# Landing pieces up to four cells wide in three slots of 32 KB, in place of three cells in four slots of 24 KB

## The chip, the cores and the metric

The kernel runs on one core of a Trainium2 chip. Its time is device microseconds (us) of one execution. Three timed runs of the kernel before took 1202.51, 1204.64 and 1207.39 us, so the median is 1204.64 us. The engines are TensorE (PE; its weight loads are PEld), VectorE (DVE), ScalarE (ACT), GpSimd (POOL) and SyncE (SP); SP only issues DMAs here. "ACTq" and "SPq" are the sequencers of ScalarE and SyncE, where DMAs are issued and semaphores waited for.

## The reference

One layer of a graph network. The adjacency matrix is dense in memory (268 MB) although it is almost empty, and every entry is used as an ordinary number:

```python
x    : (8192, 128) f32, normal        adj : (8192, 8192) f32, almost all zeros, diagonal 0.05..1
W    : (128, 128) f32

h       = max(layernorm(x, axis=-1), 0)
A_hat   = adj + eye(8192)
d       = sum(A_hat, axis=1) ** -0.5
A_norm  = d[:, None] * A_hat * d[None, :]
out     = x + relu(A_norm @ (h @ W.T))
```

The degrees `d` need the sum over a whole row of `adj` before any product with that row's part of `h @ W.T` can be taken.

## The kernel before

The matrix is cut into 16 x 16 **cells**. Cell (u, v) is rows of block u against columns of block v, 512 x 512 numbers, 1 MB. Block row u is called **stripe** u. The kernel goes through the stripes once, in order s = 0 to 15, and in stripe s it loads:

- `far[s]`: the cells right of the band (v > s + 1). They are loaded for the row sums alone. ScalarE sums them (L530) and they are thrown away. One piece takes `MOST * B` = 12 cells-wide rows of one quarter of the block rows, or several quarters when fewer cells are left (L87 to L94).
- `left[s]`: the cells v < s, in **pieces** of up to `MOST` cells (`split`, L73). VectorE transposes them (L692), TensorE multiplies the transposed cells with `support` (L485), and both VectorE (L677) and ScalarE (L540) take a part of the row sums.
- `near[s]`: the cells s and s + 1, in two buffers of their own.
- `early[s]`: cells of earlier rows that had been summed before and can now be multiplied, because the scale of their columns is known. These are loaded a second time, always three cells in a piece (L101).

After stripe 15 the cells that are still missing are loaded a second time, in pieces of up to `MOST` cells (`AGAIN_ROWS`, L107). In all the kernel reads 387 MB.

All pieces but `near` are numbered m = 0, 1, 2, ... in one list, `landing`. Piece m goes to buffer `slot[m % SLOTS]`. Both DMA queues load every piece: SP its partitions 0 to 63, ScalarE its partitions 64 to 127, two DMAs each for pieces of cells (`load_cells`, L266). A DMA's rows are n x 512 bytes long for a piece of n cells.

What sets the order: `next_piece` (L518). When ScalarE comes to piece m and it has landed, it first issues its half of piece m + `AHEAD`, and only then sums piece m. Before it issues, `load_piece` (L285) makes it wait until the piece that was in that slot has been used: `act_freed` and `dve_freed` for a piece that is summed, `t_done` (the transposes) for a second load. SP may issue its half once ScalarE has passed the same point (`act_piece`). With `AHEAD = SLOTS - 1`, the piece waited for is m - 1, in both kernels. After the last piece of a stripe, `load_kept` (L306) issues `near`, and waits first until the transposes of the column s - 1 have begun to use the other buffer. From stripe 10 on this column stands behind the first four cells of the stripe (`FIRST`, L133). After stripe 15 nothing is summed, and a slot is reloaded when the transposes of its piece are done.

VectorE transposes a cell in two halves into three buffers `adjT` (`TURNS`), so it runs at most three halves ahead of TensorE. A cell is two transposes and eight matmul instructions.

Of the kernel before, what the change touches and what calls it, by code (L numbers as in the profile page):

```python
# [28 lines left out]
def gnn_kernel(nc: bass.Bass, x: bass.AP, adj: bass.AP, w: bass.AP, out: bass.AP):  # L29
# [8 lines left out]
    C = G // Q  # L38
    CELL = N // B // NB
    BAND = 1  # L40
    MOST = 3
    SLOTS = 4
    AHEAD = 3
    HALVES = 2
    TURNS = 3
    BANKS = 5
# [26 lines left out]
    def split(first, end):  # L73

        n = end - first
        k = -(-n // MOST)
        return [(first + n * i // k, n * (i + 1) // k - n * i // k) for i in range(k)] if n > 0 else []
# [4 lines left out]
    landing = []  # L82
    far, left, again, early = {}, {}, {}, {}
    next_cell = [u + BAND + 1 for u in range(FAR_ROWS)]
    middle = []
    for u in range(NB):
        cells = NB - 1 - u - BAND  # L87
        far[u] = []
        widths = [] if cells <= 0 else [cells] if cells <= MOST * B else [MOST * B, cells - MOST * B]
        for k, width in enumerate(widths):  # L90
            per = min(B, MOST * B // width)
            for bb in range(0, B, per):
                far[u].append(len(landing))
                landing.append(("far", u, bb, min(per, B - bb), NB - cells + k * MOST * B, width))  # L94
        left[u] = []
        for v, n in split(0, u):
            left[u].append(len(landing))
            landing.append(("left", u, v, n, 0, 0))
        early[u] = []
        if u <= EARLY_TO:  # L100
            for i in range(u - MOST - BAND - 1, -1, -MOST):  # L101
                early[u].append(len(landing))
                middle.append((i, u - MOST))
                landing.append(("again", i, u - MOST, MOST, 0, 0))
                next_cell[i] = u
    AGAIN = len(landing)
    for u in AGAIN_ROWS:  # L107
# [4 lines left out]

    slot_of = [m % SLOTS for m in range(len(landing))]
    before_in_slot, landed = [], []
# [30 lines left out]
    def group(u, v):  # L145

        if v <= u + BAND:
            return "row", u
        if v >= next_cell[u]:
            return "end", AGAIN_ROWS.index(u)  # L150
        return "middle", middle.index((u, v - (v - u - BAND - 1) % MOST))

    def bank_of(g):
        kind, k = g
# [20 lines left out]
    with ctx:  # L175
# [17 lines left out]
        acc = sb("acc", [D, FAR_ROWS, G])  # L193
        slot = [sb(f"slot{i}", [P, MOST * C * CELL]) for i in range(SLOTS)]
        near = [sb(f"near{i}", [P, C, 2 * CELL]) for i in range(2)]
# [312 lines left out]
        def _(act):  # L508
# [9 lines left out]
            def next_piece(m):  # L518

                load_piece(act, (2, 3), m + AHEAD)  # L520
                if m + AHEAD in last_piece:
# [340 lines left out]
```

## Time and profile before

| | |
|---|---|
| timed runs | 1202.51 to 1207.39 us, median 1204.64 us |
| profiled execution | span 1237.8 us from first to last instruction; no time of its own beside the span |
| TensorE busy | 983.2 us (79%), 2365 instructions |
| VectorE busy | 802.4 us (65%), 965 instructions |
| ScalarE busy | 586.5 us (47%), 1735 instructions |
| DMA | 391.81 MB, mean 317 GB/s, the 16 engines busy in nearly every slice |
| granted TensorE clock, mean | 0.909 |
| cells | 256, of which 101 are multiplied before 676 us and 155 after |

How to read it: the share of an engine over the whole span hides that the kernel has two halves. The page's slices show TensorE at 3 to 8 tenths in the first half and at 9 from 700 us on, while the DMA engines show 9 nearly everywhere. "Busy" for TensorE includes the modelled ends of its matmuls. The DMA share is the time packets took, so a full queue of slow packets shows as busy as one of fast packets: the GB/s column tells them apart.

### The profile page before, as it was taken

The numbers are of one execution on the slowest core, as the hardware profiler recorded it, in microseconds if no ns is written. First come the engines' busy times: TensorE is split into PE (matmuls) and PEld (weight loads), VectorE is DVE, ScalarE is ACT, GpSimd is POOL, SyncE is SP. The second block draws the span as 40 slices with busy tenths as digits, with TensorE's granted clock in tenths as the row PEclk, the third lists the DMA queues.
The fourth block names the chain that finished last, engine by engine and source line by source line (L and its number), as shares of the span: only waits on it lengthen the run. The fifth ranks groups of instructions, "written<-read, shape, count | busy, mean of one in ns | idle before, by whom it ended". The sixth has DMA issues, their size and how long they took to land.

```text
span 1237.8 us, 9242 instructions
## 1 busy us (share of the span) xinstructions
PE 983.2 (79%) x2365; PEld 451.8 (36%) x2365; DVE 802.4 (65%) x965; ACT 586.5 (47%) x1735; POOL 52.6 (4%) x61
## 2 busy tenths in 40 slices
PE   0633346566687788796597999999999999899997
PEld 0631122222233333342243444444444444344443
DVE  5342233444476566575485888888888888778775
ACT  2797587776384637145254451724715653010011
POOL 3000000000000000000000000000000000010001
PEclk9767668678889899998798999999999999999999
DMA  9989999999999999999999999999999997999993
GB/s 301 380 320 309 392 398 362 365 369 347 362 349 343 362 337 322 314 256 274 281 291 278 329 332 360 323 276 333 309 325 320 314 271 215 271 271 348 337 328 88
DMA packets 275204, 391.81 MB, mean 317 GB/s; under 512 B 10832, under 2 KB 252624, under 8 KB 275152
## 3 DMA queue, kind: packets, MB, share of 16 engines
q1 hardware_dynamic: 137648, 195.65, 51.3%
q10 hardware_dynamic: 137504, 195.58, 50.5%
q8 instruction: 19, 0.31, 0.1%
q14 instruction: 33, 0.27, 0.1%
HBM read 386.99 MB, written 4.19 MB: 316 GB/s over the span
## 4 chain that ended last, share of the span: by engine, by line
PE 37%; DMA 8%; ACT 6%; ACTq 3%; DVE 1%; issue 0%; POOLq 0%; SPq 0%; DVEq 0%
PE bank L485 36%; DMA slot<-in_adj_dram 8%; ACT junk L540 6%; ACTq L269 2%; DVE adjT L692 1%; ACTq L277 1%; PE pre L461 0%; ACTq L315 0%; DVE near L778 0%; ACT slot L530 0%; ACT near L558 0%; DVE part L677 0%; POOLq L175 0%; PE sums_bank L449 0%; ACTq L321 0%
## 5 line engine op out<-in xcount | busy, mean ns | idle before, releaser
L485 PE MATMUL bank<-adjT,support 128*128 128x512 f32 x2048 | 936.2, 618 | 152.1 <-DVE adjT L692 150.8
L692 DVE STREAM_TRANSPOSE adjT<-slot 128x1024 f32<-128x1024 f32 x450 | 546.5, 1233 | 268.8 <-DMA slot<-in_adj_dram 157.2
L485 PEld LDWEIGHTS bank<-adjT,support 128*128 128x128 f32 x2048 | 401.8, 199 | 664.6 <-issue 661.0
L540 ACT ACTIVATE junk<-slot 128x384 bf16<-128x384 f32 (+2 forms) x540 | 254.6, 473 | 196.1 <-issue 131.3
L530 ACT ACTIVATE slot<-slot 128x6144 f32<-128x6144 f32 (+11 forms) x64 | 191.8, 2998 | 250.3 <-issue 147.8
L558 ACT ACTIVATE near<-near,dinv 128x128 f32<-128x128 f32 x64 | 20.4, 390 | 177.9 <-issue 88.5
L540 ACT ACTIVATION_READ_ACCUMULATOR junk<-slot 128x1 f32 x540 | 100.8, 187 | 0.0
L692 DVE STREAM_TRANSPOSE adjT<-near 128x1024 f32<-128x1024 f32 x62 | 74.8, 1231 | 19.0 <-PE bank L485 19.0
L540 ACT ACTIVATE junk<-near 128x256 bf16<-128x256 f32 (+1 forms) x192 | 75.5, 394 | 2.8 <-ACT junk L540 2.8
L677 DVE TENSOR_REDUCE part<-slot 128x4 f32<-128x1536 f32 (+2 forms) x45 | 69.0, 1533 | 0.0
L407 POOL TENSOR_TENSOR dinv<-total,power 128x4 f32<-128x4 f32 x16 | 16.1, 1007 | 942.0 <-DVE total L746 942.0
L449 PE MATMUL sums_bank<-by_block,spread 128*128 128x64 f32 x32 | 7.1, 310 | 50.1 <-DVE by_block L728 50.1
L428 PE MATMUL bank<-ident,acc 128*128 128x128 f32 x64 | 14.9, 378 | 31.5 <-ACT acc L515 31.5
L540 ACT ACTIVATION_READ_ACCUMULATOR junk<-near 128x1 f32 x192 | 35.8, 187 | 0.0
L436 PE MATMUL bank<-acc 128*128 128x128 f32 x128 | 23.5, 344 | 9.1 <-DVE acc L645 9.0
L718 DVE TENSOR_REDUCE folded<-part 128x16 f32<-128x32 f32 (+5 forms) x16 | 3.7, 228 | 41.3 <-ACTq L589 40.9
L449 PEld LDWEIGHTS sums_bank<-by_block,spread 128*128 128x128 f32 x32 | 6.7, 228 | 58.9 <-DVE by_block L728 53.6
L416 POOL TENSOR_TENSOR near<-near 128x512 f32<-128x512 f32 x16 | 20.3, 1270 | 174.2 <-ACT near L558 154.4
L515 ACT ACTIVATE acc<-support,acc 128x128 f32<-128x128 f32 x64 | 25.4, 479 | 2.2 <-PE bank L428 2.2
L436 PEld LDWEIGHTS bank<-acc 128*128 128x128 f32 x128 | 22.3, 261 | 9.7 <-DVE acc L645 9.7
L677 DVE TENSOR_REDUCE part<-near 128x4 f32<-128x1024 f32 (+1 forms) x16 | 18.6, 1160 | 8.0 <-DMA near<-in_adj_dram 8.0
L428 PEld LDWEIGHTS bank<-ident,acc 128*128 128x128 f32 x64 | 11.2, 198 | 32.8 <-ACT acc L515 17.5
(53 smaller groups left out, 179.1 us busy)
## 6 DMA issues: line engine op xcount, KB each, us to landing
slot<-in_adj_dram SPq DMA_DIRECT2D x118, 768.0 KB, 15.4
slot<-in_adj_dram ACTq DMA_DIRECT2D x118, 768.0 KB, 13.4
slot<-in_adj_dram ACTq DMA_DIRECT2D x56, 512.0 KB, 11.0
slot<-in_adj_dram SPq DMA_DIRECT2D x56, 512.0 KB, 12.0
slot<-in_adj_dram ACTq DMA_DIRECT2D x12, 1536.0 KB, 15.8
slot<-in_adj_dram SPq DMA_DIRECT2D x12, 1536.0 KB, 17.0
near<-in_adj_dram SPq DMA_DIRECT2D x30, 512.0 KB, 16.8
near<-in_adj_dram ACTq DMA_DIRECT2D x30, 512.0 KB, 15.2
```

Of the source, the lines that this page charges most:

```text
L269: queue.dma_start(piece(m)[b * Q:(b + 1) * Q, :, :], adj_v[u, b, :, :, v * CELL:(v + n) * CELL]).then_inc(ld_slot[slot_of[m]], 16)
L407: nc.gpsimd.tensor_tensor(dinv[:, u * R:(u + 1) * R], total[:], power[:, :R], ALU.pow).then_inc(root_ok, 1)
L416: nc.gpsimd.tensor_tensor(o[n % 2], y[n % 2], xin[n % 2], ALU.add).then_inc(o_ok, 1)
L428: ins = nc.tensor.transpose(hT_bank[b % 2][:, r * P:(r + 1) * P], h[b % 2][:, r, :], ident[:])
L436: ins = nc.tensor.matmul(sup_bank[b % 2][:, r * D:(r + 1) * D], hT[b % 2][:, r * P:(r + 1) * P], wT[:], start=True, stop=True)
L485: ins = nc.tensor.matmul(bank[bank_of(g)][:], support[:, v * R + t, :], adjT[at % TURNS][:, r, :], start=(n == first_of[g] and t == 0), st ...
L515: nc.scalar.activation(h[b % 2][:, r, :], support[:, t, :], ACT.Relu, bias=shift[:, t:t + 1], scale=rstd[:, t:t + 1]).then_inc(h_ok, 1)
L530: ins = nc.scalar.activation(far_block(m)[:, a, :], far_block(m)[:, a, :], ACT.Copy, accum_out=far_sum[u % 2][:, at:at + 1])
L540: nc.scalar.activation(junk[at % JUNKS][:, :n], cells[:, c, :], ACT.Copy, accum_out=part[u % 2][:, k, c:c + 1]).then_inc(junk_done, 1)
L558: ins = nc.scalar.activation(y[n % 2][:, r, :], y[n % 2][:, r, :], ACT.Relu, scale=dinv[:, t:t + 1])
L677: return nc.vector.tensor_reduce(part[u % 2][:, k, :most], cells[:, :most, :], AX.X, ALU.add)
L692: nc.vector.transpose(adjT[at % TURNS][:].rearrange("p t (c i) -> p t c i", i=Q), half.rearrange("p c (t r) -> p t c r", r=Q)).then_inc(t_ ...
```

## The change

Four constants are changed and one is added. `MOST` goes from 3 to 4, `SLOTS` from 4 to 3, `AHEAD` from 3 to 2. The size of a slot follows `MOST`, so it grows from 24 to 32 KB in each partition, and the slots together stay at 96 KB. `EARLY = 3` is new, and keeps the second loads within the stripes (`early`) at three cells. What `MOST` still governs becomes wider: far pieces hold up to 16 cells' width, and `left` pieces and the second loads after stripe 15 hold up to four cells.

```text
                         before                          after
pieces in all            128                             108
four-cell pieces         0                               20 (16 left, 4 after stripe 15)
far[0] (quarters x width) 4 of 1x12, 1 of 4x2            4 of 1x14
far[1]                   4 of 1x12, 1 of 4x1             4 of 1x13
far[6], far[7]           4 of 1x8, 4 of 1x7              2 of 2x8, 2 of 2x7
far[9], far[10]          2x5 2x5, 3x4 1x4                3x5 1x5, 4x4
left[4]                  2 2                             4
left[7], left[8]         2 2 3, 2 3 3                    3 4, 4 4
left[10], left[11]       2 3 2 3, 2 3 3 3                3 3 4, 3 4 4
left[12], left[13]       3 3 3 3, 2 3 2 3 3              4 4 4, 3 3 3 4
left[14], left[15]       2 3 3 3 3, 3 3 3 3 3            3 4 3 4, 3 4 4 4
early (all stripes)      18 pieces of 3                  the same
```

```diff
--- before.py
+++ after.py
@@ -38,9 +38,10 @@
     C = G // Q
     CELL = N // B // NB
     BAND = 1
-    MOST = 3
-    SLOTS = 4
-    AHEAD = 3
+    MOST = 4
+    EARLY = 3
+    SLOTS = 3
+    AHEAD = 2
     HALVES = 2
     TURNS = 3
     BANKS = 5
@@ -98,10 +99,10 @@
             landing.append(("left", u, v, n, 0, 0))
         early[u] = []
         if u <= EARLY_TO:
-            for i in range(u - MOST - BAND - 1, -1, -MOST):
+            for i in range(u - EARLY - BAND - 1, -1, -EARLY):
                 early[u].append(len(landing))
-                middle.append((i, u - MOST))
-                landing.append(("again", i, u - MOST, MOST, 0, 0))
+                middle.append((i, u - EARLY))
+                landing.append(("again", i, u - EARLY, EARLY, 0, 0))
                 next_cell[i] = u
     AGAIN = len(landing)
     for u in AGAIN_ROWS:
@@ -148,7 +149,7 @@
             return "row", u
         if v >= next_cell[u]:
             return "end", AGAIN_ROWS.index(u)
-        return "middle", middle.index((u, v - (v - u - BAND - 1) % MOST))
+        return "middle", middle.index((u, v - (v - u - BAND - 1) % EARLY))
 
     def bank_of(g):
         kind, k = g
```

The same instructions in the order of ScalarE's program, stripe 12. `L277`/`L278` are loads of far pieces, `L269`/`L270` loads of pieces of cells (`32x16x384` is three cells, `32x16x512` four), `L315`/`L316` the load of `near`; the other rows are sums. Lines after the change are one higher. Before:

```order
L277 DMA slot<-in_adj_dram 128x2x256 x4
L269 DMA slot<-in_adj_dram 32x16x384 x6
L530 ACTIVATE slot,far_sum<-slot 128x1024 x4
L269 DMA slot<-in_adj_dram 32x16x384 x2
L315 DMA near<-in_adj_dram 32x16x256 x2
L540 ACTIVATE junk,part<-slot 128x384 x12
L269 DMA slot<-in_adj_dram 32x16x384 x2
L540 ACTIVATE junk,part<-slot 128x384 x12
L269 DMA slot<-in_adj_dram 32x16x384 x2
L540 ACTIVATE junk,part<-slot 128x384 x12
L269 DMA slot<-in_adj_dram 32x16x384 x2
L540 ACTIVATE junk,part<-slot 128x384 x12
```

After:

```order
L278 DMA slot<-in_adj_dram 128x2x256 x4
L270 DMA slot<-in_adj_dram 32x16x512 x4
L531 ACTIVATE slot,far_sum<-slot 128x1024 x4
L270 DMA slot<-in_adj_dram 32x16x512 x2
L316 DMA near<-in_adj_dram 32x16x256 x2
L541 ACTIVATE junk,part<-slot 128x512 x12
L270 DMA slot<-in_adj_dram 32x16x384 x2
L541 ACTIVATE junk,part<-slot 128x512 x12
L270 DMA slot<-in_adj_dram 32x16x384 x2
L541 ACTIVATE junk,part<-slot 128x512 x12
L541 ACTIVATE junk,part<-near 128x256 x12
```

Before, three pieces (x6) are issued between the far load and the far sum of stripe 12; after, two pieces (x4). The `near` load stands in the same place, ahead of the sums of the stripe's first left piece.

The same engine at the end of stripe 4, before:

```order
L277 DMA slot<-in_adj_dram 128x2x1280
L530 ACTIVATE slot,far_sum<-slot 128x5120
L269 DMA slot<-in_adj_dram 32x16x256 x2
L530 ACTIVATE slot,far_sum<-slot 128x5120
L269 DMA slot<-in_adj_dram 32x16x256 x2
L315 DMA near<-in_adj_dram 32x16x256 x2
L530 ACTIVATE slot,far_sum<-slot 128x5120
L277 DMA slot<-in_adj_dram 128x2x1152
L530 ACTIVATE slot,far_sum<-slot 128x5120
L277 DMA slot<-in_adj_dram 128x2x1152
L540 ACTIVATE junk,part<-slot 128x256 x12
L277 DMA slot<-in_adj_dram 128x2x1152
```

After:

```order
L278 DMA slot<-in_adj_dram 128x2x1280
L531 ACTIVATE slot,far_sum<-slot 128x5120
L278 DMA slot<-in_adj_dram 128x2x1280
L531 ACTIVATE slot,far_sum<-slot 128x5120
L270 DMA slot<-in_adj_dram 32x16x512 x2
L316 DMA near<-in_adj_dram 32x16x256 x2
L531 ACTIVATE slot,far_sum<-slot 128x5120
L278 DMA slot<-in_adj_dram 128x2x1152
L531 ACTIVATE slot,far_sum<-slot 128x5120
L278 DMA slot<-in_adj_dram 128x2x1152
L541 ACTIVATE junk,part<-slot 128x512 x12
L541 ACTIVATE junk,part<-near 128x256 x12
```

The two pieces of two cells have become one of four. It is loaded where the second of the two was, after the stripe's second far sum and together with `near`; in the place of the first one the fourth far piece of the stripe is loaded, one sum later than before.

## Rows read from the trace of the kernel before

**Rows 1.** Stretches (columns: stretch, length, busy per engine (x instructions), PEclk, DMA share, GB/s).
```profile
0.00:676.00 676.00, 437.71 (x1041) 206.92 (x1041) 347.60 (x481) 390.10 (x970) 26.30 (x39) 0.84 1.03 332
676.00:1229.00 553.00, 544.85 (x1320) 244.44 (x1320) 452.85 (x481) 193.85 (x757) 23.79 (x20) 0.99 1.01 301
...
500.00:600.00 100.00, 72.07 (x155) 30.79 (x153) 52.95 (x53) 39.31 (x111) 1.01 (x1) 0.88 1.03 265
```

**Rows 2.** Waits from 0 to 676 us (waiter <- releaser: us, times, longest).
```profile
DVE adjT L692 <- DMA slot<-in_adj_dram: 153.8, 26, 15.3
...
PE bank L485 <- DVE adjT L692: 136.5, 28, 12.6
```

**Rows 3.** Waits from 676 to 1229 us.
```profile
PE bank L485 <- DVE adjT L692: 14.3, 5, 8.3
DVE adjT L692 <- DMA slot<-in_adj_dram: 13.1, 3, 9.7
```

**Rows 4.** Groups of instructions by line, 676 to 1229 us, TensorE.
```profile
L485 PE MATMUL bank<-adjT,support 128*128 128x512 f32 x1240 | 539.4, 595 | 15.6 <-DVE adjT L692 14.3 <-ACT acc L552 1.4
```

**Rows 5.** Stretches with one width of row on the queues.
```profile
126.00:146.00 20.00, 10.74 (x20) 4.99 (x20) 6.64 (x15) 10.03 (x26) 1.01 (x1) 0.59 1.02 417
334.00:348.00 14.00, 7.23 (x11) 2.75 (x10) 4.74 (x4) 3.71 (x2) 0.00 (x0) 0.76 1.07 362
387.00:397.00 10.00, 6.92 (x17) 2.82 (x16) 5.01 (x6) 0.86 (x2) 0.00 (x0) 1.00 1.10 346
930.00:945.00 15.00, 15.00 (x36) 6.65 (x35) 12.78 (x14) 5.50 (x22) 0.00 (x0) 1.00 1.07 359
```

**Rows 6.** Groups by line and shape, whole span, ScalarE's sums of far pieces.
```profile
L530 ACT ACTIVATE slot<-slot 128x6144 f32<-128x6144 f32 x12 | 63.8, 5321 | 35.1 <-issue 23.3 <-DMA slot<-in_adj_dram 10.3 <-ACT junk L540 1.5
...
L530 ACT ACTIVATE slot<-slot 128x1024 f32<-128x1024 f32 x8 | 8.3, 1044 | 23.5 <-DMA slot<-in_adj_dram 22.9 <-issue 0.6
...
L530 ACT ACTIVATE slot<-slot 128x512 f32<-128x512 f32 x8 | 4.9, 617 | 23.8 <-DMA slot<-in_adj_dram 23.1 <-issue 0.6
```

**Rows 7.** Chain, 600 to 700 us (start us, us, what): two ScalarE sums.
```profile
620.60 4.91 ACT junk L540 x24
...
627.37 6.19 ACT junk L540 x24
```

**Rows 8.** Order of time, VectorE, 673 to 680 us.
```profile
675.40 2.37 DVE L692 STREAM_TRANSPOSE adjT<-slot 128x1024 f32<-128x1024 f32 x2 [9.65 <-DMA slot<-in_adj_dram]
```

**Rows 9.** L269 issued from 1012 to 1014 us: one three-cell piece, nothing queued before it.
```profile
L269 ACTq DMA_DIRECT2D slot<-in_adj_dram x2: 604/731/858, 1012.5 to 1013.1; - x2
L269 SPq DMA_DIRECT2D slot<-in_adj_dram x2: 579/710/841, 1012.5 to 1013.1; - x2
...
DMA to landing us min/median/max: 7.0/9.2/11.1
```

**Rows 10.** Order of time, ScalarE, 440 to 472 us.
```profile
449.05 9.10 ACTq L315 DMA_DIRECT2D near<-in_adj_dram  x2
```

**Rows 11.** Order of time, ScalarE, 753 to 800 us.
```profile
759.12 4.54 ACTq L269 DMA_DIRECT2D slot<-in_adj_dram  x2
770.02 2.84 ACTq L315 DMA_DIRECT2D near<-in_adj_dram  x2
...
779.37 1.56 ACTq L269 DMA_DIRECT2D slot<-in_adj_dram  x2
...
787.43 1.56 ACTq L269 DMA_DIRECT2D slot<-in_adj_dram  x2
...
795.49 2.74 ACTq L269 DMA_DIRECT2D slot<-in_adj_dram  x2
```

**Rows 12.** Order of time, VectorE, 798 to 848 us.
```profile
820.08 1.25 DVE L692 STREAM_TRANSPOSE adjT<-slot 128x1024 f32<-128x1024 f32 x1 [0.40 <-PE bank L485]
...
830.38 1.25 DVE L692 STREAM_TRANSPOSE adjT<-slot 128x1024 f32<-128x1024 f32 x1 [0.40 <-PE bank L485]
...
842.39 4.63 DVE L692 STREAM_TRANSPOSE adjT<-slot 128x1024 f32<-128x1024 f32 x4 [1.71 <-DMA slot<-in_adj_dram]
```

## The prediction

> **What bounds the kernel now.** I read the stretches first. Up to 676 us TensorE is busy 438 of 676 us and the DMA share is 1.03; from 676 us on TensorE is busy 545 of 553 us, at a DMA share that is still 1.01 [rows 1]. The waits say the same: in the first part VectorE waits 153.8 us for landing pieces and TensorE 136.5 us for VectorE [rows 2]; in the second part these are 13.1 and 14.3 us [rows 3]. So the time before is 676 us in which the queues set the pace, and 553 us in which TensorE does: 1240 matmul instructions, eight to a cell, are 155 cells, and 553 / 155 = 3.57 us a cell [rows 4]. A second taken from the first part shows in the end time. In the second part only a new wait of TensorE does, and a gain of the queues is worth nothing there.
>
> The second part is not far from the other bound. A cell of three-wide pieces is 1.05 MB, and at 359 to 362 GB/s [rows 5] takes 2.9 us, against TensorE's 3.57; but each stripe adds `near` and a far piece that feed TensorE little or nothing. So the queues have some per cent to spare, and idle time on them beyond that turns into waits of TensorE.
>
> The profiled span, 1237.8 us, is 33 us over the median of the runs, 1204.64. The stretch 500 to 600 us moved only 265 GB/s at a share of 1.03 [rows 1], where the same kind of pieces moves 360: slow packets, not missing ones. I take the sum below as a difference to the span (1237.8 + x) and carry x over to the median.
>
> **The change part by part.**
>
> *Wider rows before 676 us.* Rows of 1024 B moved at 346 GB/s, of 1536 B at 359 to 362, the long rows of far pieces at 417 [rows 5]. Rows of 2048 B do not stand alone anywhere. Bounds: 362 (no gain over three cells) and 417 (as far rows). I take 370, near the row of the nearest width. A piece of 4.19 MB then takes 11.3 us (11.6 and 10.1 at the ends), one of three cells (3.15 MB) 8.7, one of two (2.10 MB) 6.1. Stripe 4: 12.2 becomes 11.3, 0.9 saved. Stripe 7: 20.9 becomes 20.0, 0.9. Stripe 8: 23.5 becomes 22.6, 0.9. Stripe 10: 29.6 becomes 28.7, 0.9. Together 3.6 us, with the five pieces at the ends 2.1 and 9.6. Far cells: 2.1 MB of stripe 0 go from 1024 B rows to 7168 B rows, 6.1 to 5.0 us; stripe 1 has 1.05 MB of 512 B rows, which I price as 1024 B rows, 3.0 to 2.5. That is 1.6 us. On ScalarE, which is late there, four sums of 1044 ns and four of 617 become wider sums elsewhere: a sum's price is 190 ns plus 0.835 ns a column (5321 and 1044 ns) [rows 6], so only the 8 x 0.19 = 1.5 us go; half of that I put on the path. Sum: -6 us, ends -3 and -12. Merging far pieces in stripes 6 and 7 leaves rows and bytes as they were: 0.
>
> The Trainium skill, page DMA: Bandwidth & Descriptors, section Where 436 GB/s comes from, has loads from HBM bound at about 358 GB/s a core; by it rows over 1024 B would be worth 3% at most. The trace does not agree: 417 GB/s over 20 us [rows 5].
>
> *The first piece of stripe 11.* At 675.40 VectorE starts on a piece of two cells that it had waited 9.65 us for, and from there TensorE hardly stops [rows 8]. After the change this piece has three cells and lands (3.15 - 2.10) MB / 362 GB/s = 2.9 us later: +2.9 us, ends 0 (if TensorE is full earlier) and +3.
>
> *One piece less in flight, first part.* Before, ScalarE at piece m issues m + 3 while m + 1 and m + 2 are on the queues; after, m + 2 while only m + 1 is. A three-cell piece issued onto an empty queue landed 11.1 us after its last DMA's issue at 1013.1, the first being issued at 1012.5: 11.7 us, of which the bytes are 8.7 and 3.0 are latency [rows 9]. So the queue stays full only if ScalarE comes to piece m less than (time of m + 1) - 3.0 us after its landing: 5.7 us of room for three cells, 8.3 for four, about 3 for the far pieces of stripes 3 to 5. ScalarE's work fits: a sum over three cells takes 6.19, over two 4.91 us [rows 7], so four would be 7.5 us (each cell adds 1.28), plus 1.5 us to issue (779.37) [rows 11], against 8.7 and 11.3 us on the queues. And part of its lateness goes away: with more than two pieces queued an issue blocks, 9.10 us for the `near` of stripe 8 (449.05) [rows 10], 4.54 us for a third piece (759.12) [rows 11]. Nine stripe ends are left where `near` (waits for a column) or a free slot makes it late. Ends: 0, and the full 3.0 us at each of nine ends, +27. I take half a microsecond an end: +4.
>
> *One slot less, second part.* This is the largest term. At a stripe's end come three early pieces, the far piece of the next stripe, then its left pieces A and B. The far piece holds a slot and gives TensorE nothing. With three slots A may be issued once the second last early piece is transposed, B once the last one is. VectorE ends these two 10.3 us apart (820.08 and 830.38, the last transposes of the two pieces before stripe 13) [rows 12]. A is wanted when the last early piece is through: 10.3 us after its issue, and it needs 11.7 us with three cells, 11.3 + 3.0 = 14.3 with four. Late by 1.4 or 4.0. With four slots it had one piece more, 10.3 us, to spare. Stripe 11 is 3, 4, 4: A 1.4, B then another 2.6. Stripe 12 is 4, 4, 4: A 4.0, then B has 13.8 us and is in time. Stripe 13 is 3, 3, 3, 4: A 1.4, and B, issued 10.3 us after A and wanted 10.3 us after A landed, is in time. Together 9.4 us; stripes 14 and 15 have no far piece. VectorE's lead of up to three halves over TensorE absorbs what is under about 2 us once, but the queues in this part also have slow spells: at 842.39 even four slots ran dry for 1.71 us [rows 12]. I take +8, ends +2 and +15. ScalarE's place does not matter here: its `near` issue in stripe 12 already waits from 763.7 (759.12 + 4.54) to 770.02, and stands at the same sum after the change [rows 11].
>
> *After stripe 15* the widths are 2, 3, 1, 2, 3, 2, 2, 3, 3, 2, 3, 3, then 4, 3, 4, 3, 4, 4. A slot is asked for again after three pieces. A three-cell piece behind two pieces of three cells together has 3 x 3.57 = 10.7 us plus what VectorE leads, against 11.7; all others have over 14. 0, end +3.
>
> *Nothing:* ScalarE's fewer sums and VectorE's nine fewer L677 lie under the queues in the first part and under TensorE in the second.
>
> Sum: -6 + 2.9 + 4 + 8 = +9. Span 1247, timed 1213.6; I say 1213.
>
> **The rivals.** *A, gains and losses cancel:* the width gain is 6 to 8 us and the stalls of the second part are swallowed by VectorE's lead, -7 + 3 + 2 + 2 = 0: about 1205. For it: only 20 of 108 pieces have four cells, and all early pieces stay at three, so the change reaches little on either side.
>
> *B, faster:* four-cell rows go at the rate of far rows, -12, ScalarE freed from blocked issues keeps the queue as full as before, and left pieces of four arrive with as much room as three did: -12 + 2.9 + 1 + 1 = -7, about 1197. It decides from 400 GB/s on in stretches of four-cell pieces. Against it: 1024 to 1536 B brought under 5% [rows 5]. In a sentence of its own: the Trainium skill, page Perfetto Trace Analysis, section DMA Optimizations, says that DMAs under 2 KB carry much overhead and that batching them up helps dramatically; the step from 346 to 362 GB/s is this trace's measure of it.
>
> *C, much slower:* a slot less makes the queue dry at every stripe end, because ScalarE stands blocked before the `near` issue (6.3 us in stripe 12) with one piece in flight instead of two. From a block of 5.7 us on the queue dries; nine stripe ends at 3 us and six at 4 less the 6 gained give about +40, 1245. Against it: the block stands only from stripe 10 on, and the piece in flight there has four cells.
>
> *That it doesn't do what it says* is excluded by the order of ScalarE's program: four-cell loads are there.
>
> **How the numbers follow.** A measurement of this kernel can tell about 0.5% (6 us) from no change. Forecast 0.38, its own range 1211 to 1226; A 0.32; B 0.22; C 0.08. The range of 8 in 10 takes all of A, half of B and none of C: 1197 to 1231. Faster (under 1198.6) 0.22, within 0.5% 0.33, slower 0.45 (forecast and C, less the lower edge of the forecast).
>
> **What would show it.** Width: a stretch of four-cell pieces alone, 370 GB/s (B: over 400). Depth, first part: the waits of VectorE for pieces before the last turn to TensorE-bound stay near 150 us; C has them over 180. Second part: waits of VectorE for `slot` pieces over the last 155 cells go from 13 us to 20 or more, in rows at the first left pieces of stripes 11, 12 and 13; if they are not there, the largest term is wrong. If the turn comes more than 5 us earlier and the waits stay at 13, B is right. A change of the rate of three-cell pieces, which no term here has, would make all of it wrong.

## The result, and the profile after

The changed kernel took 1235.74 us (median of 4 runs, 1231.32 to 1240.91), the kernel before in the same comparison 1206.01 us (4 runs, 1202.51 to 1207.39): a ratio of 1.0249, 95% interval 1.0203 to 1.0294. The same kernel again (run e13 below) took 1231.70 us, ratio 1.0201 (1.0103 to 1.0299). The forecast was 1213 us, 1197 to 1231: the side is right, the size is not. Some 30 us were lost and 8 forecast.

The profiled execution of before that the prediction rests on had a span of 1237.8 us. A second one of the same kernel (run e0) has 1207.6, and the stretch with 265 GB/s [rows 1] moves 337 there. All comparisons below are with this second one. Its stretches, cut where TensorE begins to be full (653 us) and around the part after stripe 15:

```profile
0.00:653.00 653.00, 441.53 (x1054) 209.97 (x1055) 353.95 (x489) 396.06 (x978) 26.30 (x39) 0.84 1.04 347
653.00:1208.00 555.00, 540.42 (x1313) 242.88 (x1312) 449.32 (x478) 190.42 (x757) 26.29 (x22) 0.99 1.01 297
500.00:600.00 100.00, 86.38 (x195) 37.78 (x195) 71.64 (x75) 46.75 (x140) 2.01 (x2) 0.93 1.07 337
1003.00:1141.00 138.00, 133.39 (x338) 61.06 (x338) 107.39 (x137) 13.00 (x41) 13.65 (x11) 0.99 1.05 298
```

The same view of the changed kernel (columns as in [rows 1]). The next three stretches hold mostly four-cell pieces, and answer to [rows 5]; the last holds long far rows with a two-cell piece among them:

```profile
0.00:683.00 683.00, 466.06 (x1106) 219.66 (x1107) 372.28 (x503) 393.12 (x898) 27.33 (x40) 0.84 1.02 343
683.00:1239.00 556.00, 525.82 (x1261) 234.32 (x1259) 429.56 (x451) 170.06 (x607) 25.33 (x21) 0.98 0.96 283
1022.00:1172.00 150.00, 138.31 (x337) 62.40 (x338) 107.46 (x137) 12.68 (x40) 12.43 (x10) 0.95 0.99 277
...
447.00:467.00 20.00, 15.40 (x27) 6.25 (x26) 8.30 (x8) 5.60 (x4) 0.00 (x0) 0.76 1.06 369
655.00:675.00 20.00, 19.72 (x46) 9.11 (x47) 17.34 (x25) 2.52 (x10) 1.01 (x1) 0.92 1.06 370
742.00:750.00 8.00, 8.00 (x21) 3.78 (x20) 6.11 (x9) 0.00 (x0) 1.01 (x1) 0.91 1.05 360
...
130.00:150.00 20.00, 9.55 (x16) 3.90 (x16) 4.35 (x4) 11.97 (x5) 0.00 (x0) 0.67 1.03 391
```

The reader is to see two things. The price of four-cell rows was about right: 369, 370 and, in a shorter stretch, 360 GB/s, where 370 was taken. And in the third row, from 1022 to 1172 us, in a part that the prediction priced at nothing, TensorE stands for 12 of 150 us (before, for 4.6 of 138), and the same instructions (337 and 338 in the records) are busy for 138.3 us where they took 133.4 before. The waits, first part and second, answering to [rows 2, 3], and then, of the second part, what falls after stripe 15 (from 1022 us):

```profile
PE bank L486 <- DVE adjT L693: 149.8, 24, 17.8
DVE adjT L693 <- DMA slot<-in_adj_dram: 144.1, 15, 20.8
...
DVE adjT L693 <- DMA slot<-in_adj_dram: 28.7, 8, 8.9
...
PE bank L486 <- DVE adjT L693: 22.1, 11, 7.5
...
DVE adjT L693 <- DMA slot<-in_adj_dram: 16.2, 5, 5.7
```

In e0 VectorE's waits for pieces are fewer than in [rows 2, 3]: 120.6 us up to 653 us, and 0.7 us in all the rest.

```profile
DVE adjT L692 <- DMA slot<-in_adj_dram: 120.6, 21, 15.4
```

To see where the time goes I take, in each profile, when TensorE starts the first of the eight matmul instructions of a cell, cells counted in the order of the program. The order of the 256 cells is the same in all kernels here. The rows are us against run e0, whose own times stand first:

| run | cell 40 | 83 (stripe 10) | 101 (11) | 123 (12) | 146 (13) | 203 (rest) | 223 | 240 | last end |
|---|---|---|---|---|---|---|---|---|---|
| e0, before | 392.1 | 574.5 | 646.9 | 725.1 | 804.5 | 1003.1 | 1081.3 | 1141.4 | 1198.3 |
| after | +8.6 | +11.2 | +8.4 | +15.3 | +18.7 | +19.0 | +25.4 | +31.0 | +31.5 |
| e13, after again | +1.5 | +5.3 | +1.1 | +8.6 | +13.8 | +14.1 | +19.8 | +27.1 | +27.1 |
| e1, three slots of three | +18.3 | +27.1 | +28.1 | +34.7 | +36.9 | +46.6 | +55.2 | +57.5 | +59.6 |
| e7, far as before | +16.2 | +23.8 | +20.9 | +28.3 | +32.5 | +32.8 | +42.1 | +48.3 | +49.2 |
| e17, far joined as before | +5.3 | +10.8 | +8.2 | +16.5 | +21.0 | +21.2 | +30.0 | +36.6 | +38.0 |
| e6, three slots first | +26.4 | +28.7 | +29.4 | +29.4 | +29.4 | +29.2 | +27.7 | +29.3 | +31.3 |
| e3, rest in threes | +6.6 | +7.1 | +3.1 | +10.3 | +14.3 | +15.0 | +21.3 | +23.6 | +25.1 |
| e11, stores later | -1.1 | +0.7 | -3.5 | +3.0 | +6.9 | +7.2 | +5.7 | +12.2 | +12.2 |
| e16, both of these | -2.4 | -0.7 | -5.1 | +1.0 | +5.3 | +5.6 | +4.1 | +5.1 | +5.1 |
| e10, three slots in the rest | +3.3 | +2.0 | -1.2 | -1.7 | -1.6 | -1.5 | +5.8 | +8.8 | +10.4 |
| e15, both kernels | +4.8 | +3.4 | -2.4 | -3.3 | -3.3 | -3.8 | -3.6 | -3.6 | -3.6 |

Five of these profiles (after, e13, e3, e11, e16) run the same program up to stripe 11, and stand there between -5.1 and +8.4, median +1.1. So a difference of several us between two single profiles in this part, which the queues bound, can be the execution's own. From stripe 11 on the five agree: from cell 101 to 203 they lose 10.6, 13.0, 11.9, 10.7 and 10.7 us.

### The profile page after: what moved, and what is told of

Same layout as the page of the kernel before. It is cut to its first block, busy times and chain, and to the rows that moved or that the text cites. A ratio compares the mean times of both kernels' runs of the same rounds, so it can differ in the third digit from the quotient of the medians.

```text
span 1239.1 us, 8874 instructions
## 1 busy us (share of the span) xinstructions
PE 991.9 (80%) x2365; PEld 454.0 (37%) x2365; DVE 801.8 (65%) x954; ACT 563.2 (45%) x1503; POOL 52.7 (4%) x61
## 4 chain that ended last, share of the span: by engine, by line
PE 43%; DMA 17%; DVE 4%; ACTq 1%; ACT 1%; issue 1%; SPq 1%; POOLq 0%; POOL 0%; DVEq 0%
PE bank L486 42%; DMA slot<-in_adj_dram 16%; DVE adjT L693 3%; DMA out_dram<-near 1%; ACTq L316 1%; ACTq L270 1%; ACT junk L541 0%; DVE part L678 0%; ACT near L559 0%; ACT slot L531 0%; PE pre L462 0%; SPq L270 0%; DVE near L779 0%; SPq L322 0%; SPq L329 0%
## 5 line engine op out<-in xcount | busy, mean ns | idle before, releaser
L486 PE MATMUL bank<-adjT,support 128*128 128x512 f32 x2048 | 946.9, 624 | 171.9 <-DVE adjT L693 171.9
L693 DVE STREAM_TRANSPOSE adjT<-slot 128x1024 f32<-128x1024 f32 x450 | 547.5, 1234 | 299.8 <-DMA slot<-in_adj_dram 172.8
L486 PEld LDWEIGHTS bank<-adjT,support 128*128 128x128 f32 x2048 | 406.0, 201 | 690.6 <-issue 685.5
L541 ACT ACTIVATE junk<-slot 128x384 bf16<-128x384 f32 (+3 forms) x432 | 234.4, 544 | 206.8 <-issue 131.1
L531 ACT ACTIVATE slot<-slot 128x7168 f32<-128x7168 f32 (+13 forms) x56 | 190.2, 3397 | 247.3 <-issue 119.9
L693 DVE STREAM_TRANSPOSE adjT<-near 128x1024 f32<-128x1024 f32 x62 | 74.0, 1226 | 15.4 <-PE bank L486 15.4
L541 ACT ACTIVATION_READ_ACCUMULATOR junk<-slot 128x1 f32 x432 | 80.6, 186 | 0.0
L678 DVE TENSOR_REDUCE part<-slot 128x4 f32<-128x1536 f32 (+3 forms) x36 | 68.0, 1888 | 0.0
L429 PE MATMUL bank<-ident,acc 128*128 128x128 f32 x64 | 14.3, 367 | 31.8 <-ACT acc L516 31.8
L450 PE MATMUL sums_bank<-by_block,spread 128*128 128x64 f32 x32 | 6.6, 291 | 21.2 <-DVE by_block L729 21.0
L646 DVE COPY acc<-bank 128x512 f32<-128x512 f32 x16 | 10.9, 685 | 18.7 <-PE bank L429 18.7
L779 DVE TENSOR_TENSOR near<-bank,acc 128x128 f32<-128x128 f32 x56 | 14.7, 378 | 12.6 <-PE pre L462 8.6
L429 PEld LDWEIGHTS bank<-ident,acc 128*128 128x128 f32 x64 | 10.7, 192 | 33.0 <-ACT acc L516 18.1
## 6 DMA issues: line engine op xcount, KB each, us to landing
near<-in_adj_dram ACTq DMA_DIRECT2D x30, 512.0 KB, 16.5
```

The source lines that it names most:

```text
L429: ins = nc.tensor.transpose(hT_bank[b % 2][:, r * P:(r + 1) * P], h[b % 2][:, r, :], ident[:])
L486: ins = nc.tensor.matmul(bank[bank_of(g)][:], support[:, v * R + t, :], adjT[at % TURNS][:, r, :], start=(n == first_of[g] and t == 0), st ...
L531: ins = nc.scalar.activation(far_block(m)[:, a, :], far_block(m)[:, a, :], ACT.Copy, accum_out=far_sum[u % 2][:, at:at + 1])
L541: nc.scalar.activation(junk[at % JUNKS][:, :n], cells[:, c, :], ACT.Copy, accum_out=part[u % 2][:, k, c:c + 1]).then_inc(junk_done, 1)
L678: return nc.vector.tensor_reduce(part[u % 2][:, k, :most], cells[:, :most, :], AX.X, ALU.add)
L693: nc.vector.transpose(adjT[at % TURNS][:].rearrange("p t (c i) -> p t c i", i=Q), half.rearrange("p c (t r) -> p t c r", r=Q)).then_inc(t_ ...
```

## The experiments

All times below are medians; "before" lay at 1205.9 to 1211.1 in each comparison.

**The kernel before again (e0)**, for a profile to compare with.

> The kernel before, unchanged, for a second profile. Its first profile had a span of 1237.8 us beside timed runs of 1202.5 to 1207.4, and only 265 GB/s from 500 to 600 us. If that stretch was a disturbance, the span is now about 1205 and the stretch moves 330 to 350 GB/s; TensorE's idle time from 500 to 610 us falls from 31 to 15 us or less. If it belongs to the kernel, the span is 1235 again and only the profiler slows it.

Measured: 1209.4, span 1207.6, and the rows above: the slow spell of [rows 1] was that execution's own.

**The depth alone (e1) and the moment of asking alone (e2).**
```
e1: the changed kernel with MOST = 3     (pieces as before, SLOTS = 3, AHEAD = 2)
e2: the kernel before with AHEAD = 2     (pieces as before, SLOTS = 4)
```


> The changed kernel with pieces of three cells again (MOST = 3), in three slots of 24 KB, AHEAD = 2: the depth of the queue alone. Theory 1, one piece less in flight and one slot less cost it all, and wide rows gave back some 6 us: ratio to before 1.03 (1240 us), slower than the change. Theory 2, the loss comes from wide pieces, which land later and are given back later as a whole, and depth costs little: ratio 1.00 to 1.01.

> The kernel before with AHEAD = 2 and its four slots of three cells: one piece less in flight, but the slot waited for is that of the piece two back, so no wait for a slot. If the load is lost by issuing later (fewer bytes queued), ratio 1.02 to 1.03 as with three slots. If it is lost by the wait for the slot, that is for VectorE and TensorE to be done with piece m - 1, ratio 1.00.

Measured: e1 1261.2, ratio 1.0482 (1.0423 to 1.0540); e2 1213.1, ratio 1.0065 (1.0033 to 1.0096). A slot less and asking one piece later cost 55 us together at three cells, asking later alone 8. The two differ only in the slot that is waited for, so most of the loss is the wait for a slot that VectorE and ScalarE must first give back, not the later place in ScalarE's program. The page's group for VectorE's transposes, before (e0) and in e1, shows for whom it waits (busy, mean ns | idle ahead of them, and how much of it the pieces ended):

```profile
L692 DVE STREAM_TRANSPOSE adjT<-slot 128x1024 f32<-128x1024 f32 x450 | 547.6, 1234 | 234.4 <-DMA slot<-in_adj_dram 121.3
```
```profile
L693 DVE STREAM_TRANSPOSE adjT<-slot 128x1024 f32<-128x1024 f32 x450 | 546.5, 1233 | 321.7 <-DMA slot<-in_adj_dram 210.1
```

The wait for landing pieces grows by 89 us. In the changed kernel it is 172.8 us (144.1 + 28.7), in the middle. Wide pieces thus give some 26 us back over the whole kernel (55 less 30), four times what was forecast.

**Where the width pays (e7, e17).**
```
e7:  widths and per of the far pieces with EARLY (3) in place of MOST (4)
e17: per = max(1, min(B, EARLY * B // width))    (rows of 14 and 13 cells stay, no merging)
```


> The changed kernel with its far pieces cut as before (12 cells wide at most: rows of 6 KB and 1 KB in stripe 0, and more pieces), its left pieces still up to four cells wide. With three cells everywhere and three slots TensorE came to stripe 4 (cell 20) 10 us later than in the changed kernel, to stripe 11 20 us later. If the far pieces' widths make those 10 us: 1243 to 1250. If they are worth what the prediction gave them (1.6 us and some ScalarE): 1236 to 1239.

> The changed kernel with its long rows of 14 and 13 cells in stripes 0 and 1, but the shorter far pieces cut as before: stripes 6 and 7 in four pieces of 2 and 1.75 cells of room and not in two of 4 and 3.5, stripes 9 and 10 as before too. If the rows' width makes the 22 us by which the kernel with all far pieces cut as before is slower, it stays near the changed kernel, 1230 to 1240. If it is that a small piece leaves most of one of three slots empty, so that less is on the way, part of the loss comes at stripes 6 to 10: 1244 to 1254, late by the cells from 40 to 83.

Measured: e7 1258.0, ratio 1.0446 (1.0409 to 1.0483); e17 1247.0, ratio 1.0321 (1.0276 to 1.0366). At stripe 11 the ladder is e1 +28.1, e7 +20.9, e17 +8.2, changed kernel +1.1 (the median of five). By these profiles left pieces of four cells are worth 7, the long rows of stripes 0 and 1 13, the merged far pieces of stripes 6, 7, 9 and 10 another 7. Each step is a difference of single profiles, and the steps of 7 are within the spread above. The timed medians have the same order, with steps of 3 (the intervals of e1 and e7 overlap), 11, and 11 to 15 us. So the long rows and the merging are worth something; that the wider left pieces are is not shown. Merging changed no row and no byte where it joins whole blocks, and was priced at nothing. An explanation that fits, and was only argued: a piece of 2 cells takes a whole slot, so that with three slots only some 2 MB stand behind the piece that is landing.

**Which part keeps a loss (e6).** The kernel before with `slot_of`: m % 3 up to the first left piece of stripe 11, then m % 4. (e6, e5 and e10 write their slots as places in one buffer, at the addresses that three or four slots of three cells have. Where e5 and e10 use all four, they are within 4.2 us of e0 in the table's measure.)

> The kernel before, with three of its four slots used up to the first left piece of stripe 11, and four from there. With three slots throughout, TensorE came to stripe 11 28 us late. If a second of the first part shows in the end time, as the prediction has it, 1230 to 1237. If the second part catches up when it has four slots, because it isn't bound by TensorE alone, under 1225.

Measured: 1237.0, ratio 1.0238 (1.0206 to 1.0270). It is 29.4 us late at stripe 11 and 29.2 at cell 203: with four slots the second part gives back nothing of a loss in the first. That step of the prediction stands.

**The part after stripe 15: widths (e3), slots (e5, e10), stores (e11), and both cures (e16).**
```
e3:  for v, n in split(next_cell[u], NB, EARLY)      (most = 3 after stripe 15)
e5:  before; slot_of = m % 4 if m < AGAIN else m % 3
e10: before; slot_of = m % 4 if m < AGAIN else (2, 3, 0)[(m - AGAIN) % 3]
e11: SyncE:  while stored < done_by(m - 1):          (was done_by(m))
e16: e3 and e11
```


> The changed kernel with the loads after stripe 15 in pieces of at most three cells; all else as changed. In the changed kernel's trace TensorE is idle 7.2 us from 1100 to 1229 us, where three four-cell pieces land just when VectorE waits for them; before it was 0.0. Theory 1: with three slots these waits go with the width, 5 to 7 us faster than the change, ratio to before 1.019. Theory 2 (the end is bound by TensorE whatever the width): same as the change, 1.025.

> The kernel before, with three of its four slots of 24 KB used for the pieces after stripe 15, and four up to there. The prediction put this at nothing (0 to 3 us: 1206 to 1209). With three slots throughout, the stretch after stripe 15 was 13 us longer (57.7 from cell 203 on in the kernel before, against three slots, start to end): if that is the slot's own price there, 1216 to 1221.

Measured: e3 1231.5, ratio 1.0200 (1.0143 to 1.0258), 10.1 us lost after cell 203, 2 to 3 less than the changed kernel's 12.5 and 13.0. Its time alone, beside 1235.7 and 1231.7, doesn't tell. e5 1235.7, ratio 1.0222 (1.0181 to 1.0263), more than either theory had: 10.9 of its 29 us came before cell 203, where its first piece takes the slot of the piece just ahead of it. Hence e10:

> The kernel before with three of its four slots for the pieces after stripe 15, as in the earlier run of this kind, but the first of them now takes the slot that comes free first (there it took the slot of the piece just ahead of it, and TensorE lost 11 us by it). If the missing slot has a price of its own in this part, 15 to 18 us stay: 1219 to 1225. If the earlier run's loss was that change of slots, under 1212.

Measured: 1222.0, ratio 1.0128 (1.0060 to 1.0196); 11.9 us lost after cell 203 (-1.5 to +10.4). The time is in the expected 1219 to 1225, the loss below the expected 15 to 18 us and far from the 0 of the prediction. The slot has a price of its own there even with pieces of three cells. The order of time on three engines of the changed kernel shows one half of what it consists of. First ScalarE's queue, then SyncE's, then VectorE (start, us, what [idle ahead <- releaser]):

```profile
1080.56 1.79 ACTq L270 DMA_DIRECT2D slot<-in_adj_dram  x2
```
```profile
1087.18 0.81 SPq L329 DMA_DIRECT2D out_dram<-near  x2
1088.04 0.94 SPq L322 DMA_DIRECT2D near<-in_x_dram  x2
1089.02 1.01 SPq L329 DMA_DIRECT2D out_dram<-near  x2
1090.07 0.99 SPq L322 DMA_DIRECT2D near<-in_x_dram  x2
1091.16 5.98 SPq L270 DMA_DIRECT2D slot<-in_adj_dram  x4
```
```profile
1105.33 3.50 DVE L693 STREAM_TRANSPOSE adjT<-slot 128x1024 f32<-128x1024 f32 x3 [5.68 <-DMA slot<-in_adj_dram]
```

Piece 98's slot was free at 1080.4. ScalarE asked for its half at 1080.56. SyncE stands until 1087.18 for a result to store, issues two stores and two loads of x, and asks for its half at 1091.16, 10.6 us later. The piece lands at 1105.3 and VectorE has waited 5.68 us. In the kernel before SyncE is as late (piece 115: 1061.8 and 1072.9), but a fourth slot stands between that and VectorE, which doesn't wait.

> The changed kernel, but SyncE issues each store of the last part one piece later, behind a piece's loads, as ScalarE does for its half of it: in the profile of the changed kernel SyncE came to some pieces 3 to 10 us after ScalarE, since it waited for a result to store. If that wait makes the 12.5 us that the part after stripe 15 lost, 1222 to 1230. If the missing slot does, it stays within 4 us of the changed kernel: 1231 to 1237.

> The changed kernel with pieces of up to three cells after stripe 15 and with SyncE's stores one piece later. Stores alone gave 16 us back (1219.5), three cells alone 4 (1231.5). If both take away the same wait, 1215 to 1220; if they add up, 1213 to 1216. What is left over the kernel before is then the start of stripes 11 to 13, which the prediction had at 8 us.

Measured: e11 1219.5, ratio 1.0120 (1.0087 to 1.0153). Its profile loses 5.0 us after cell 203 where the changed kernel lost 12.5 and 13.0. The medians lie 12 to 16 us apart, and the four runs of e11 don't overlap with the eight of the changed kernel. In the traces the rest lies before stripe 11, where the two run the same program; why all four runs have it isn't shown. Here the same piece 98, in the run e11:

```profile
1067.67 1.62 SPq L270 DMA_DIRECT2D slot<-in_adj_dram  x2
1075.11 0.81 SPq L329 DMA_DIRECT2D out_dram<-near  x2
```
```profile
1085.23 3.50 DVE L693 STREAM_TRANSPOSE adjT<-slot 128x1024 f32<-128x1024 f32 x3 [0.76 <-DMA slot<-in_adj_dram]
```

SyncE asks at the moment ScalarE does, ahead of its stores, and the wait is 0.76.

The other half is the width. Piece 102 is the first of four cells after stripe 15. Both engines ask for it at the same moment (1123.07 in the changed kernel, 1105.4 in e11), another piece being on its way, and it lands 26.4 and 23.6 us later. VectorE waits for it in both (the changed kernel, then e11):

```profile
1149.50 4.63 DVE L693 STREAM_TRANSPOSE adjT<-slot 128x1024 f32<-128x1024 f32 x4 [5.07 <-DMA slot<-in_adj_dram]
```
```profile
1129.01 3.50 DVE L693 STREAM_TRANSPOSE adjT<-slot 128x1024 f32<-128x1024 f32 x3 [5.95 <-DMA slot<-in_adj_dram]
```

With pieces of three cells at most, VectorE stands for 0.5 us or less at this place (e3, e16).

Measured for e16: 1224.2, ratio 1.0140 (1.0067 to 1.0214), a median above the expected 1215 to 1220, in a comparison in which before spread from 1201 to 1246 too. Its profile is of its fastest run (1216.2) and loses nothing after cell 203 (+5.6 to +5.1), so in this trace the stores and the width together are the whole loss of this part. Its three other runs took 1223.4 to 1225.4, and why is not explained. What its profile has left is the +10.7 of stripes 11 to 13.

**The spread of one execution (e13).** The changed kernel, unchanged.

> The changed kernel, unchanged, on the chip of the three runs beside it. In its own profile it was 8.4 us late at stripe 11, in two profiles of kernels that have the same program up to there 3.1 us late and 3.5 us early. If that is the spread of one execution, this profile lies between -4 and +9 at stripe 11, and 8 to 12 us more are lost in stripes 11 to 13 and 5 to 13 after stripe 15; time 1230 to 1240.

Measured: 1231.7; +1.1 at stripe 11, then 13.0 to cell 203, 13.0 after it.

**The same memory in places of one cell (e8, e4, e9).**
```
slot    -> ring [P, 12 cells];  piece m starts at start_of[m] (a table), takes ceil(its cells)
waits   -> for every earlier piece whose places overlap;  issue: up to m + AHEAD, where room is
e8: pieces of after, AHEAD 4    e4: pieces of before, AHEAD 4    e9: pieces of before, AHEAD 3
```


> The changed kernel, with its three slots of 32 KB turned into twelve places of one cell in the same 96 KB: 45 of 108 pieces find room for a fourth piece or more, no piece has fewer than three. Its pieces keep their widths. Theory depth (the loss of the change is the slot that is missing): a third to two thirds of the 30 us come back, 1216 to 1226. Theory coarseness (a piece of four cells is late because it is long, and holds its place long): under 8 us come back, 1228 to 1236.

> The kernel before, with its four slots of 24 KB turned into twelve places of one cell (8 KB) in the same 96 KB: every piece takes as many places as it has cells, so that beside pieces of one and two cells a fifth fits (41 of 128 pieces find room one piece or more earlier than before, none later). If what counts is how early the next loads can be asked for, 3 to 12 us faster than before (1194 to 1203). If four slots are deep enough already, 1204 to 1208.

> The kernel before with twelve places of one cell and its pieces laid so that each finds room at least four pieces ahead, as in the run with the fifth piece, but ScalarE asks for piece m + 3 again when it comes to piece m, not for m + 4. If the fifth piece's issue, on which ScalarE stands blocked with its sums behind it, made that run over 40 us slower, this one is at 1198 to 1209. If the places themselves do (pieces side by side in other rows of the memory), it is over 1230.

Measured: e8 1236.7, ratio 1.0259 (1.0196 to 1.0322). Depth expected 1216 to 1226 and that didn't come; coarseness expected 1228 to 1236, which is nearer. Its profile has -3.1 at stripe 11, within the spread, and 21.8 us lost after cell 203 (10.8 of them from cell 240 on). e4 ran from 1248 to 1331 (median 1325.6), e9 from 1201 to 1335 (median 1260.6), with no interval. Neither theory is borne out: one execution of e9 was at 1201.3 with nothing unusual in its profile, others 50 to 130 us over it with the same program. In e4's profile ScalarE's time ahead of far sums without a releaser in the profile was 245.4 us over the span, against 109.3 in e0, but the queues were slower as well (268 GB/s from 400 to 640 us; e9 339). Why these two scatter so stays open; no conclusion rests on them.

**Both kernels' pieces together (e12, e18, e15).**
```
e12: pieces of after up to stripe 10, of before from stripe 11; twelve places; AHEAD 3
e18: the kernel before with SyncE's done_by(m - 1)
e15: e12 and e18
```


> Both kernels together: up to stripe 10 the pieces of the changed kernel (four cells, far pieces of 16), from stripe 11 on those of the kernel before, in twelve places of one cell, ScalarE asking for three pieces ahead where there is room. Up to stripe 10 a piece finds room three pieces ahead or more, from stripe 11 on four. Additive theory: first part 0 to -4 us against the kernel before (as measured with the changed kernel's pieces in twelve places), second part 0: 1200 to 1207. If wide pieces cost in the first part what three slots do there, 1214 or more.

> The kernel before with SyncE's stores one piece later, nothing else. With four slots TensorE stood for only 4.6 us after stripe 15, and SyncE's loads of a piece were up to 11 us behind ScalarE's without being wanted yet: 1201 to 1207. If the version with twelve places owes its 0.6% to the stores, the low end; if to the places, 1205 to 1207.

> The run of both kernels together (1203.6, twelve places of one cell), with SyncE's stores one piece later as well. With four pieces ahead TensorE stood for only 5 us after stripe 15, so there is little to take back: 1197 to 1203. If stores one piece later make the last results late, 1204 or more.

Measured: e12 1203.6, ratio 0.9987 (0.9963 to 1.0012); e18 1205.4, ratio 0.9982 (0.9959 to 1.0004); e15 1201.6, ratio 0.9941 (0.9902 to 0.9979). Only e15's interval is clear of one: 0.6% faster than the kernel before, and 2.4% under the changed one on the same chip. The 0.6% rests on a comparison in which before scattered (1201 to 1246), so that e15 is at least as fast as the kernel before is what can be said; neither of its two halves is faster by itself. In its waits from 640 us on, VectorE waits for a piece once, for 1.3 us:

```profile
PE bank L501 <- DVE adjT L709: 7.0, 4, 2.3
DVE adjT L709 <- DMA ring<-in_adj_dram: 1.3, 1, 1.3
```

## Why the prediction was wrong

By its own terms, forecast beside measured:

| term | forecast | measured |
|---|---|---|
| wider rows and pieces, first part, with the wider first piece of stripe 11 | -6 (-3 to -12) + 2.9 | -27 (e1 against the changed kernel's median, at stripe 11) |
| one piece less in flight, first part | +4 (0 to +27) | +28 and +29 (e1, e6) |
| one slot less, stripes 11 to 15 | +8 (+2 to +15) | +10.6 to +13.0 (five profiles) |
| after stripe 15 | 0 (0 to +3) | +12.5 and +13.0 |

**The step that failed is "After stripe 15 ... 0, end +3".** It compared 10.7 us and VectorE's lead with the 11.7 us that a lone piece took from its first issue [rows 9], and so assumed that both halves of a piece are asked for when its slot comes free, and that a piece takes as long as a lone one. The first assumption left out what stands on SyncE's queue between the slot's coming free and the issue: the stores, which wait for results. The kernel before shows it too (in e0 SyncE asks 2.8 to 11.1 us after ScalarE for eleven of the last thirteen pieces), but as a lag that nobody waited for. Four slots hid it, and the change took the cover away. Moving the stores took 7 to 8 of the 13 us back, pieces of three cells 2 to 3 by themselves, and both together, in one trace, all of it. The second assumption fails as clearly: four-cell pieces did not take 14.3 us from issue to landing. The three of stripe 12 took 20 to 22 (asked for at 718.9, 729.3 and 739.1, landed at 739.0, 750.7 and 761.5), with another piece on its way. Piece 102 took 26.4, against the 6 x 3.57 = 21.4 us for which the two pieces before it keep TensorE busy: the prediction counted it among those with time to spare. Even the 11.7 us of [rows 9] were not quite those of an empty queue, since the piece before landed at 1013.7, 1.2 us after the issue.

**The two terms of the first part were each too small by a factor of four or more, and cancelled.** "Half a microsecond an end" was a choice inside 0 to +27, argued from ScalarE's free time; it was the wrong end (28 and 29 are just above the upper one), since what is late is mostly the slot (e2 against e1), not ScalarE. "Merging far pieces ... 0" was wrong too. That the net of the first part came out near the forecast (-27 + 28 beside -6 + 2.9 + 4) is luck. What the two errors share, as far as the runs show it: the queues were reckoned in bytes and rates, and not in how much is asked for ahead of the piece that is landing. Three slots with small pieces in them lose 28 us; three slots of fuller ones are as good as four of three cells, +1.1 us within the spread. Rival C had the loss of depth, but with a return of only 6 us from wider pieces, and by another cause, ScalarE blocked before `near`, which the prediction saw only from stripe 10 on: 18 of e1's 28 us are lost before cell 40 (stripe 7). Its own sum, nine ends at 3 and six at 4 less 6, gives +45 and not +40.

**The largest term was right in size, and nearly in place.** From cell 101 to 123, where it had 2.6 + 4.0 us (the second piece of stripe 11, the first of stripe 12), the five profiles lose 6.1 to 7.5, but all of it at the first piece of stripe 12, where VectorE waits 7.8 to 9.4 us; at the second of stripe 11 it waits 0.3 us at most. From 123 to 146 they lose 3.4 to 5.2, forecast 1.4 for stripe 13; then, to cell 203, 0.3 to 0.7. VectorE's rows at the first left piece of stripe 12 and at the first two of stripe 13; in e0 it has no wait at the first of either:

```profile
739.04 2.37 DVE L693 STREAM_TRANSPOSE adjT<-slot 128x1024 f32<-128x1024 f32 x2 [8.87 <-DMA slot<-in_adj_dram]
```
```profile
821.81 2.37 DVE L693 STREAM_TRANSPOSE adjT<-slot 128x1024 f32<-128x1024 f32 x2 [2.35 <-DMA slot<-in_adj_dram]
833.25 2.37 DVE L693 STREAM_TRANSPOSE adjT<-slot 128x1024 f32<-128x1024 f32 x2 [1.30 <-DMA slot<-in_adj_dram]
```

The sign of the prediction came from this term. The waits that it named as its test (from 13 to 20 or more) went to 28.7, but 16.2 of these fall after stripe 15, in the part priced at nothing; 12.5 are in the rows above. "Near 150 us" in the first part was 144.1, which looked like a confirmation of +4 and was two large terms cancelling; beside e0's 120.6 it isn't even near. A sum of waits doesn't tell such a pair apart; only the kernel with one of them did.

## What to carry to other kernels

When landing slots are traded for piece size, count what is asked for ahead of the landing piece, stage by stage, with the small pieces at their real size in their slot. Take the time from asking to landing from a piece that has another ahead of it, not from a lone one. Then list, for every engine that issues half of a transfer, what else stands in its queue between the slot's coming free and the issue: idle time there is free only as long as the depth covers it. A range as wide as 0 to +27 in a term is a reason to look for the row that settles it, not to choose near one end.

## What the runs showed of the hardware

A pause of TensorE of 7.5 us cost more than its length. In the order of time on TensorE around the wait at stripe 12 (start, us, what), and in the stretches around it (granted clock third from the right):

```profile
724.61 8.32 PE L486 MATMUL bank<-adjT,support 128*128 128x512 f32 x19
740.43 4.77 PE L486 MATMUL bank<-adjT,support 128*128 128x512 f32 x7 [7.50 <-DVE adjT L693]
```
```profile
722.00:732.00 10.00, 10.00 (x25) 4.46 (x24) 6.82 (x7) 1.16 (x3) 0.00 (x0) 1.00 1.06 315
740.00:744.00 4.00, 3.57 (x5) 1.71 (x6) 3.02 (x7) 0.00 (x0) 0.00 (x0) 0.56 1.05 357
744.00:748.00 4.00, 4.00 (x13) 1.97 (x12) 3.64 (x7) 0.00 (x0) 1.01 (x1) 1.00 1.06 358
1105.00:1110.00 5.00, 3.28 (x4) 1.51 (x5) 3.50 (x3) 0.00 (x0) 0.00 (x0) 0.53 1.08 331
```

Before the pause an instruction takes 438 ns (8.32 / 19) at full clock, 2.4 GHz; the seven after it take 681 ns (4.77 / 7), at a granted 0.56, near the level of 1.2 GHz, and from 744 us the clock is full again. So 7.5 us of waiting cost about 1.7 us more (7 x 0.243). From 1105 to 1110 us, behind the wait for piece 98, the granted clock is 0.53. The part from 1022 to 1172 us is 12 us longer than before (150 against 138). Slower instructions make 4.9 of these (138.3 - 133.4), which no term of the prediction had.

The loss of the first part with three slots shows mostly as packets that took longer, and less as DMA engines without work. The rows are from 95 us to stripe 11 (cell 101), in e0, e1 and e6:

```profile
95.00:647.00 552.00, 400.33 (x845) 174.11 (x845) 304.91 (x335) 329.36 (x866) 9.06 (x9) 0.85 1.05 349
```
```profile
95.00:675.00 580.00, 397.80 (x842) 172.05 (x840) 304.14 (x333) 331.37 (x871) 9.06 (x9) 0.84 1.04 335
```
```profile
95.00:676.00 581.00, 397.13 (x841) 172.11 (x840) 304.46 (x332) 331.90 (x871) 9.06 (x9) 0.84 1.03 334
```

The last column, GB/s, falls by 4%, the one before it, the share, by 1 to 2%. Length times share is the time that packets took on one DMA engine: 580 us in e0, 603 and 598 in the other two, for nearly the same bytes (rate times length, 193 and 194 MB). Counted from the packets in the traces, fewer than eight were in flight for 5.9 us of the stretch in e0, 13.1 in e1 and 16.4 in e6. So a queue that is nearly dry is 7 to 11 of the 28 and 29 us. Whether the packets took longer because fewer were asked for isn't shown: both executions with three slots have it, but the first profile of the kernel before had a slow spell of packets with four. The stretch's length is what to read, not the share.
